# An attention and feed-forward layer on one Trainium2 core: the projection moved behind the second feed-forward layer, and eleven bursts per head, short and long in turn

## The reference, cut to what matters

```python
def _L0_attn_ref(x, Wq, bq, Wk, bk, Wv, bv, Wo, bo):      # B, N, D, H = 4, 2048, 256, 16
    split = lambda t: t.reshape(b, n, H, Dh).transpose(0, 2, 1, 3)
    q = _rope(split(x @ Wq + bq)); k = _rope(split(x @ Wk + bk)); v = split(x @ Wv + bv)
    scores = jnp.einsum('bhnd,bhmd->bhnm', q, k) / jnp.sqrt(jnp.float32(d))
    weights = jax.nn.softmax(scores, axis=-1)
    inter = jnp.einsum('bhnm,bhmd->bhnd', weights, v)
    return inter.transpose(0, 2, 1, 3).reshape(b, n, d) @ Wo + bo

def _L0_ffn_ref(x, k0, k1, k2, s0, s1, s2):               # weights are +1 or -1
    h = jnp.concatenate([x, -x], axis=-1)
    h = jax.nn.relu(s0 * _conn_dense(k0, h)) * 2           # to 1024 features
    h = jax.nn.relu(s1 * _conn_dense(k1, h)) * 2           # to 1024 features
    return s2 * _conn_dense(k2, h)                         # to 256 features

xn = _layernorm(x, axis=-1)
x = x + _L0_attn_ref(xn, ...) + _L0_ffn_ref(xn, ...)
```

## Time and profile before

| | |
|---|---|
| median of 3 runs | 2842.97 us (2841.0 to 2846.34) |
| profiled execution | 2845.93 us, its span 2844.1 us |
| PE busy | 2647.0 us, 93% of the span |
| ACT busy | 2095.7 us, 74% |
| DVE busy | 1092.7 us, 38% |
| granted TensorE clock over the span | 0.966 of full |

### The profile page before, as it was taken

The page is one execution under the profiler, slowest core; times in us unless marked ns, Lnnn a source line. Parts: engine busy times, 40 slices in busy tenths (PEclk is TensorE's granted clock), DMA queues, the critical chain, the costliest instruction groups (busy, mean ns, idle before and its releaser), DMA issues.

```text
span 2844.1 us, 49497 instructions
## 1 busy us (share of the span) xinstructions
PE 2647.0 (93%) x20423; PEld 1337.2 (47%) x20423; DVE 1092.7 (38%) x1689; ACT 2095.7 (74%) x2301; POOL 378.0 (13%) x309
## 2 busy tenths in 40 slices
PE   6787299999999999999999999999999999999997
PEld 3443144544454445454545444454455454444444
DVE  7999532323332324232322333232423223232322
ACT  4445278888888787887878687878878787878783
POOL 5888400000000000000000000000000000000000
PEclk9889699999999999999999999999999999999998
DMA  6666521222121212121212222121312122222213
GB/s 198 191 196 194 155 54 50 57 50 57 50 57 49 63 45 74 48 68 51 56 57 55 72 57 68 47 67 48 81 48 57 56 55 62 57 72 55 65 39 100
DMA packets 279701, 211.74 MB, mean 74 GB/s; under 512 B 183616, under 2 KB 227392, under 8 KB 272960
## 3 DMA queue, kind: packets, MB, share of 16 engines
q1 hardware_dynamic: 271040, 200.30, 25.8%
q10 hardware_dynamic: 8448, 8.39, 0.9%
HBM read 132.08 MB, written 76.55 MB: 73 GB/s over the span
## 4 chain that ended last, share of the span: by engine, by line
PE 80%; DMA 4%; DVE 2%; issue 1%; SPq 1%; POOL 1%; ACT 0%; POOLq 0%; DVEq 0%
PE ps_o L911 32%; PE ps_f L946 24%; PE ps_s L896 21%; DMA y<-rest_sum_d 3%; PE ps_f L959 2%; DMA heads_t<-heads 1%; POOL heads L1020 1%; DVE h_lo L1077 1%; DVE h_hi L1075 1%; PE ps_f L1001 0%; DMA q_rows<-row_shift 0%; DVE sums L1041 0%; SPq L797 0%; DMA probs<-rest_sum_d 0%; SPq L813 0%
## 5 line engine op out<-in xcount | busy, mean ns | idle before, releaser
L876 ACT ACTIVATE probs<-ps_s 128x1024 f32<-128x1024 f32 x2048 | 1935.5, 1034 | 533.5 <-PE ps_s L896 531.3
L911 PE MATMUL ps_o<-probs,v_ones 128*32 128x512 f32 x8192 | 1011.2, 600 | 0.0
L896 PE MATMUL ps_s<-q_rows,k_rows 50*128 50x512 f32 x4096 | 853.0, 437 | 33.5 <-DMA q_rows<-row_shift 32.7
L896 PEld LDWEIGHTS ps_s<-q_rows,k_rows 50*128 50x128 f32 x4096 | 366.5, 184 | 698.0 <-ACT probs L876 605.9
L1075 DVE TENSOR_SCALAR h_hi<-ps_f 128x512 fp32r<-128x512 f32 x224 | 154.4, 689 | 973.8 <-PE ps_f L946 973.7
L946 PE MATMUL ps_f<-h_hi,ffn_w 64*128 64x512 f32 x2048 | 406.1, 393 | 0.0
L946 PE MATMUL ps_f<-h_lo,ffn_w 64*128 64x512 f32 x2048 | 405.1, 391 | 0.0
L911 PEld LDWEIGHTS ps_o<-probs,v_ones 128*32 128x32 f32 x8192 | 200.6, 108 | 417.4 <-issue 321.8
L1020 POOL TENSOR_TENSOR heads<-heads,sums 128x512 f32<-128x512 f32 x64 | 82.5, 1289 | 2213.3 <-DVE sums L1041 2213.3
L1041 DVE RECIPROCAL sums<-sums 128x128 f32<-128x128 f32 x256 | 229.0, 926 | 1.7
L946 PEld LDWEIGHTS ps_f<-h_lo,ffn_w 64*128 64x128 f32 x2048 | 194.9, 186 | 37.9
(11 more groups left out here) (95 smaller groups left out, 1524.1 us busy)
## 6 DMA issues: line engine op xcount, KB each, us to landing
k_rows<-k_parts SPq DMA_DIRECT2D x128, 256.0 KB
q_rows<-q_parts SPq DMA_DIRECT2D x384, 64.0 KB
q_parts<-parts SPq DMA_DIRECT2D x32, 512.0 KB, 3.7
k_parts<-parts SPq DMA_DIRECT2D x32, 512.0 KB, 4.5
k_rows<-k_parts SPq DMA_DIRECT2D x128, 128.0 KB
x_chunk<-in_x ACTq DMA_DIRECT2D x16, 512.0 KB, 4.0
xn_t<-xnT SPq DMA_DIRECT2D x16, 512.0 KB, 4.5
v_heads<-v_sb SPq DMA_DIRECT2D x16, 512.0 KB, 5.2
```

The lines of the kernel that those rows point to most:

```text
L876: nc.scalar.activation(probs[:, s % PBUF, half * 2 * C:(half + 1) * 2 * C], ps_s[:, half].rearrange("p c n -> p (c n)"), ACT.Exp, scale=SC ...
L896: last = nc.tensor.matmul(ps_s[:, half, w], k_rows[rows, u, t * P:(t + 1) * P], q_rows[rows, u, half], start=True, stop=True)
L911: last = nc.tensor.matmul(ps_o[32 * c:32 * c + 2 * DH], v_ones[:, u, t], probs[:, s % PBUF, c * C:(c + 1) * C], start=(t == 0), stop=(t == ...
```

## The change

Three things are altered, all by the table.

1. `BURSTS` was ten rounds per head (2, 1, 2, 2, 1, 2, 1, 2, 2, 1), six long and four short. It is now eleven, short and long in turn and a short one at the end: 1, 2, 1, 2, 1, 2, 1, 2, 1, 2, 1. The three visits of a long round now get 3, 4 and 2 of the pairs in place of 3, 3 and 2, and the last short round of a head has one visit. SECOND's phases now have 5 or 6 visits and THIRD's 2 or 3, so that some phases begin behind the first or the second visit of a round, where in SECOND and THIRD each began with a round before.
2. The projection goes from round 6 of the pass (in its first head, between FIRST and SECOND) to round 37 (in its fourth head, between SECOND and THIRD). SECOND's carry is `xT[:, 1]` now, so that `headsT` stays free for it.
3. SP loads the next pass's `xT` at j = 2 and only when SECOND is done, `split` follows at step 58 in place of 44, and the store of a head goes ahead of these waits.

```diff
-SPLIT_AT = 44
+SPLIT_AT = 58
-PROJECT_AT = 6
-BURSTS = (2, 1, 2, 2, 1) * 2
+BURSTS = (1, 2) * (KT // 3) + (1,)
+PROJECT_AT = 3 * len(BURSTS) + 4
...
-    weights = [3, 3, 2] * (BURSTS.count(2) * HEADS)
-    counts = [[1, 2] * (FT // 2), [6] * FT, [3] * TT]
+    weights = ([3, 4, 2] * (KT // 3) + [3]) * HEADS
+    counts = [[1, 2] * (FT // 2), [5] * 6 + [6] * 2, [3, 2, 3, 2]]
...
-        n = 3 if count == 2 else 0
+        n = 3 if count == 2 else 1 if first % KT == KT - 1 else 0
...
-PROJECT_PLACE = FT + 1
+PROJECT_PLACE = 2 * (FT + 1)
...
-        carry = (xT[:, 0], headsT[:, 0])
+        carry = (xT[:, 0], xT[:, 1])
...
+                    if j >= 1:
+                        store_head(i, j - 1)
-                    if j == 1 and not last:
+                    if j == 2 and not last:
                         sp.wait_ge(xT_split, i + 1)
-                        sp.wait_ge(group_used, outs_before(i, projects) + place(projects, FIRST, FT) + 1 + BANKS)
+                        sp.wait_ge(group_used, outs_before(i, projects) + place(projects, SECOND, FT) + 1 + BANKS)
```

More of the change, by code:

```diff
@@ L116, in place @@
 def place(projects, layer, phase):
-    if layer == FIRST:
-        return phase
-    return (FT + 1) * layer + phase + (TT if projects else 0)
-PROJECT_PLACE = FT + 1
+    return (FT + 1) * layer + phase + (TT if projects and layer == THIRD else 0)
+PROJECT_PLACE = 2 * (FT + 1)
 OUTS = (place(False, THIRD, TT) + 1, place(True, THIRD, TT) + 1)
@@ L832, in one_pass @@
                         sp.dma_start(y_out[b - 1, r], y[:]).then_inc(y_stored, 16)
-                    if j >= 1:
-                        store_head(i, j - 1)
                 sp.wait_ge(group_used, outs_before(i, projects) + OUTS[projects] + BANKS)
```

## The result

The changed kernel takes 2816.85 us (median of 4 runs, 2815.70 to 2817.59), the kernel before 2841.98 us in the same comparison (2840.68 to 2846.34). The ratio is 0.9909, with a 95% interval of 0.9891 to 0.9926: 0.9% faster, where 2813 was forecast, within 2788 to 2832. The profiled execution of the changed kernel took 2815.7 us, its span is 2813.9.

The account below looks back on a forecast made before the run. PE, in order and busy 93% of the span, was taken as the bound. Terms of -72.2, +12.2, +22.1, +7.2 and +0.9 sum to -29.8 us, taking the median from 2843 to 2813, range 2788 to 2832.

Parts of the forecast that it names:

- The projection moved: Projection, 12 passes: moved later, it no longer waits for y or runs at a slow clock; -72.2 us.
- Rival B: Projection: its tiles stay at 5.2 us though the data is there; 2834 us in all, chance 8%.
- The bursts: Rounds of every pass: more short rounds and late phase begins, less waiting for ACT; +12.2 us, bounds 0 to 22.
- The end of each head: Next head's first weigh: waits 0.35 us for DVE's copy of ps_o, 63 times; +22.1 us, bounds 0 to 38.
- rival A: Heads' ends: they cost nothing, so the terms of 22 and 7 fall; 2784 us, chance 8%.
- The end of each pass: Next pass's first pair: waits 0.48 us for DVE's third-layer takes, 15 times; +7.2 us, bounds 0 to 15.
- the tail: Kernel's end: the third layer's takes stand 0.88 us ahead of the last reciprocals; +0.9 us.
- Rival C: Heads' ends: DVE is not free; at 1.2 us per head the kernel is slower, 2867 us, chance 6%.
- DMAs: Later xT load: DVE may stand some 3 us in the split of passes without projection, hidden by slack; no cost.
- so the median goes from 2843 to 2813: Last step: the profiled execution lay 3 us above the median, so the summed gain was taken off the median.

Follow-up runs that it names:

- The bursts alone: Eleven rounds per head as in the change, but the projection stays between first and second layer; against the kernel before: 2818.22 us, ratio 0.9908.
- long first: Changed kernel with rounds 2, 1, ..., 2, 1, 1, the last short round's visit between its score pairs, takes ahead of the copy: 2787.78 us, ratio 0.9800.
- the move alone: Kernel before, its ten rounds per head kept, with projection between second and third layer and carry, xT load, split as changed: 2776.38 us, ratio 0.9761.
- The lengthened wait: Changed kernel, but a head's first weigh also waits for DVE's shuffle behind the copy: 2871.05 us, ratio 1.0099.

## Why the prediction was right, point by point

**The projection moved** was the largest term, -72.2 us. Per pass it was to add 3.35 us in place of 9.37. It adds 151.87 - 148.33 = 3.54, so the term is -70.0, 2.2 us short. The tiles take 3.65 us with the way into them, and 3.5 was taken from the last batch's. There was no new wait at the second layer's end, as DVE's 3.21 us said. Rival B, a slow clock for another reason, is out: the clock is 1.00 from 1000 to 2600 us, and all 12 projections take the same time.

One thing in this part isn't borne out, though it doesn't touch the sum. The move was named as what takes the wait away. The bursts alone do it as well (2818.22), because they end the reciprocals sooner and bring the projection later. The sum holds in spite of it, since the wait can go only once. But the 72 us belong to the move only where the old bursts stay.

**The bursts**, +12.2: the plain pass grew by 2.62 us, of which heads' ends are 3 x 0.34 + 0.49 = 1.51 and the banks 0.28. So 0.83 is left for the bursts, 13.3 us in 16 passes, and long first against the move alone gives 11.4. A phase's begin behind another visit costs 0.19 us rather than 0.15: rounds with nine pairs take 3.41 us to their weigh with one and 3.22 without (medians of 48 and 32). Two such rounds of pass 3, the first without, the second with:

```profile
860.11 0.50 PE L894 MATMUL ps_s<-q_rows,k_rows 50*128 50x512 f32 x2
...
862.77 0.40 PE L944 MATMUL ps_f<-h_hi,ffn_w 64*128 64x512 f32 x2
863.01 0.39 PE L894 MATMUL ps_s<-q_rows,k_rows 50*128 50x512 f32 x2
863.33 1.93 PE L909 MATMUL ps_o<-probs,v_ones 128*32 128x512 f32 x16
...
866.84 0.50 PE L894 MATMUL ps_s<-q_rows,k_rows 50*128 50x512 f32 x2
...
870.25 1.92 PE L909 MATMUL ps_o<-probs,v_ones 128*32 128x512 f32 x16
```

The fourth score pair follows the ninth pair by 0.24 us, so it waits no more, as forecast. The forecast's upper bound for this part was worked out too low: 0.3 us per begin gives 0.76 + 6 x 0.15 = 1.66 us per pass, 26.6 us and not 22. By the rule of the Trainium skill that the forecast weighed here ("TensorEngine Tiling (Array Packing)", "Key Properties"), taken as a full last pair at each switch, the added rounds would cost 7 us more and the part 19. The 13.3 and 11.4 measured for the whole part speak against this price. They don't speak against the drain itself, which the forecast's 0.21 per round may hold.

**The end of each head**, +22.1: 48 x 0.34 and 15 x 0.49, which is 23.7, 1.6 more. The 0.49 has the fourth wait's 0.15 in it, which the forecast didn't see. The lengthened wait and long first show that it is the path, and rival A (2784) falls with it.

**The end of each pass**, +7.2: the first pair's wait for the banks is 0.28 us and not 0.48, since the weigh ahead of it is itself some 0.15 later than forecast. That makes 4.2 us, 3.0 less. In the tail the reciprocals end 5.64 us after the copy's start in place of 5.02, so +0.6 where 0.9 was forecast, but what comes behind them varies by more than that. Rival C didn't come true: the copy starts 1.20 or 1.21 us after the last weigh does at 63 of the 64 heads' ends, and 1.56 us once.

**DMAs**, nothing: DVE has no wait for `xT` within the passes. Nor did it stand the 3 us that the forecast thought possible in passes without projection, for the 12.8 us to landing did not stay: the median is 3.5 us now. It goes with the load's new place: 3.6 us with the move alone, 13.1 with the bursts alone.

**From the profile to the median.** The terms add up to -28.8 by the measured sizes, the tail left out, and to -29.8 by the forecast's. They agree so well by some luck: the projection, the bursts and the heads' ends turned out 4.9 us dearer together, the passes' ends 3.0 us cheaper, and the tail's 0.9 is not counted. The two profiled executions are 30.2 us apart (2845.93 and 2815.70), and the time forecast for the profiled one was 2816. The 1.4 us between 28.8 and 30.2 lie outside of these terms and stay open. The medians are only 25.1 us apart. The step that was off is the last one, "so the median goes from 2843 to 2813". The profiled execution of before lay 3 us above its median. The runs of each kernel without the wait for `y` lie within 0.4 to 2.7 us of each other, and those of before went from 2837.4 to 2849.1 over all experiments. Within its own trace the projection rounds went from 8.84 to 12.20 us. Where the part that is removed is the part that varies, the time after is the profiled time less what its own trace shows, 2816, and not the median less the same. That the executions of before differ by just this wait is inferred, as only one of them was profiled.

## What to carry to other kernels

A change made of two parts should be costed part by part, even when their sum comes out right: here one part (the move) is worth 67 us by itself and the other costs 40 on top of it, and the best kernel of the study (2776.38 us) is the one that leaves the second out. Both parts should be run alone too, for their worths need not add up: each took the same wait away, and behind the bursts the move gained 1.4 us. When bursts are reordered, look at what stands between the last use of an accumulator and its first reuse: 0.34 us or more there, 63 times, cost 23.7 us, and all the rest of the new bursts 11.4 to 13.3. A forecast made from one profiled execution should be set against the median with care where a wait that varies is what goes.

## What the runs showed of the hardware that was not expected

- A wait that has long been met is not always free: PE started 0.25 or 0.26 us after the releasing copy with four waits on the matmul, and 0.10 or 0.11 with three, some 0.15 us at each such place.
- A phase's begin that waits on PE's own last matmul of the phase before cost 0.19 us of PE's time even with a score pair between.
- The time of a projection whose data is there is the same to 0.01 us in all 12 passes: 4.31 or 4.32 us from the round's start to the weigh, in the changed kernel, with the bursts alone and with long rounds first.
